# Routing six token tiles of batch 0 to expert slots, and masking six of eight local attention tiles on the vector engine

## Chip, cores and metric

One core of a Trainium2 chip runs the kernel. The metric is the device time of one execution in microseconds (us); lower is better. The engines are PE (matrix products), ACT (scalar functions), DVE (vector operations) and POOL (general operations); SP issues most of the DMAs. Each engine works through its own list of instructions in order and waits on semaphores that others raise.

## The reference, cut to what matters

Input x is 2 batches x 1024 tokens x 128 channels, in fp32. First comes layer norm, an attention of 16 heads of 8 channels and a projection with residual; then layer norm and a gated network of eight experts, of which each token uses two:

```python
# attention: each query sees the 64 keys up to itself, and pooled keys of four levels
As = [S[:, :, qg, kg].reshape(bh, n, m)]          # the local band of 64 keys
...
# gated network
gate_scores = softmax(einsum('btd,ed->bte', x, Wg))
topk_val, topk_idx = top_k(gate_scores, 2)
topk_val = topk_val / (topk_val.sum(axis=-1, keepdims=True) + EPS)
comb = (one_hot(topk_idx, E) * topk_val[..., None]).sum(axis=-2)
for e in range(E):
    a, b = split(einsum('btd,hd->bth', x, W1[e]) + b1[e], 2)
    eo = einsum('bth,dh->btd', a * sigmoid(b), Wo) + bo
    out = out + eo * comb[..., e:e + 1]
```

An expert that a token did not choose has the weight zero in `comb`, so computing all eight for each token and computing only the two chosen give the same output.

## The kernel before

**The order of work** is one list, `schedule()`, written out by hand. Every engine walks the same list (`for step in SCHEDULE`) and does its own part of each step. So a step's place in the list is its place in the order of each engine, and an engine that waits in one step holds up all its later steps.

**Attention** runs in eight units, `u` = 0 to 7: batch `u // 4` and a group of four heads. A unit has ten score steps, `("score", u, i)`. Steps 0 and 1 score all queries against pooled keys (L1289, 8 products each). Steps 2 to 9 score local tile k = i - 2, two windows of 64 queries for four heads: PE first puts the barring values into the bank, a product of 512 columns with the identity (L1303), so that exp gives zero outside the band; then it adds two score products of 256 columns (L1306). ACT takes exp of the bank (L868). Three steps behind, `("out", u, k)` multiplies the probabilities with the values: 16 passes for the local part (L1327) and 4 for the pooled part (L1331). `BARRED_BY_PE` says for which k PE bars; before, it is all eight. For the others DVE has a `mask` step, a minimum of the probabilities with a band that holds the largest number inside and zero outside; before, it never runs. The masks stand in the list one score step behind the score. There are three score banks and a ring of five probability buffers.

Beside these, the list `beside` places other work at a unit and step: projections of q, k, v for later units, the `guard` and `shift` steps of the next unit, and from unit 5 on what ends batch 0: `rden` (DVE's reciprocal of the denominators, L1072), `spread` (DVE multiplies the outputs with reciprocals that went to memory and back, L1078, the DMAs are L576 and L578 in `load_reciprocals`), `proj`, layer norm (`stat2`, `apply2`), `x2T` (transposes), `gatelog` (logits, four steps of six small products) and `gate` in four parts (DVE's top two and weights, L950 to L974). `w1` prepares one expert's weights: POOL subtracts (L724), ACT copies the high part (L841), DVE takes the low part (L1096). `values` lets POOL spread the values of the next half unit (L658, four copies).

**The gated network** follows: 16 tiles of 128 tokens x 8 experts = 128 `hidden` steps. PE makes three products of 512 columns, split in high and low parts (L1140 to L1142), ACT the sigmoid of half of it (L893), DVE the product with the token's weight for this expert (L1123) and POOL adds the experts up (L752). Hidden banks form a ring of five, the temporaries `gtmp` another of five. In the next tile's steps 5 and 7 PE transposes the sum (`hidT`, L1255) and multiplies with the output weights (`y`, L1271). The steps that end batch 1 (`rden`, `spread`, `proj` and so on up to `gate`) are spread over tiles 0 to 7.

**The DMA queue of SP** has its own order, by unit: keys and head queries of the next unit, queries and pooled keys of the one after, weights, and `gather_outputs`, each behind its waits.

## Time and profile before

| | us |
|---|---|
| median of 3 runs | 288.18 (287.26 to 295.06) |
| the profiled execution, time | 288.01 |
| its span, first to last instruction | 286.2 |

Busy in the span: PE 273.4 us (96%), DVE 154.6 (54%), ACT 154.7 (54%), POOL 135.8 (47%). The mean granted clock of PE was 0.964 of full speed. Matrix products overlap their neighbours, so the distance from one start to the next start is what counts for PE, not the printed length of one. PE at 96% busy says that it has few gaps, not that it is at its peak. A length printed for another engine is that of one instruction, or of a run of equal ones with their count behind the x.

### The profile page before, as it was taken

To read this page: it belongs to the slowest core of one execution; us is meant where nothing else is said; L and a number is where in the kernel's file an instruction comes from. 1 tells how busy PE (TensorE), PEld (TensorE's weight loads), DVE (VectorE), ACT (ScalarE), POOL (GpSimd) and SP (SyncE) were. 2 spreads that over 40 slices of the span, in tenths; PEclk is the share of its full clock that TensorE was granted. 3 is DMA by queue.
4 is the path that set the end of the run, shared out by engine and by line. 5 is a ranking of instruction groups with operands and counts; after the bars stand their busy time and mean duration, and the time that the engine had idled before them with its cause. 6 is when DMAs were issued, how large, how long until landed. Compare 5 with 4: busy or idle time off the path is not lost.

```text
span 286.2 us, 7298 instructions
## 1 busy us (share of the span) xinstructions
PE 273.4 (96%) x2705; PEld 226.5 (79%) x2705; DVE 154.6 (54%) x453; ACT 154.7 (54%) x316; POOL 135.8 (47%) x235
## 2 busy tenths in 40 slices
PE   7999999999999999993999999999999999999994
PEld 6868767887788988883888888788888678888883
DVE  7782644633344001322643162789886987777773
ACT  6765745534653432742487456544676555555551
POOL 7753302300041154140171301888885678888881
PEclk9999999989999975998999799999999999999999
DMA  7221176340097687558445011300000000000000
GB/s 212 61 58 60 57 171 192 81 126 2 11 289 277 168 229 170 145 155 165 128 144 154 26 22 21 85 10 10 10 11 9 10 11 10 9 11 18 11 9 19
DMA packets 19683, 24.14 MB, mean 84 GB/s; under 512 B 8312, under 2 KB 14456, under 8 KB 19648
## 3 DMA queue, kind: packets, MB, share of 16 engines
q1 hardware_dynamic: 18528, 22.80, 28.8%
q10 hardware_dynamic: 1120, 0.89, 1.2%
q8 instruction: 21, 0.34, 0.5%
q14 instruction: 14, 0.11, 0.1%
HBM read 11.91 MB, written 5.37 MB: 60 GB/s over the span
## 4 chain that ended last, share of the span: by engine, by line
PE 88%; DVE 3%; issue 3%; DMA 2%; SPq 1%; ACT 1%; POOL 1%; DVEq 0%; ACTq 0%; POOLq 0%
PE bank L1327 13%; PE bank L1140 12%; PE bank L1142 11%; PE bank L1141 11%; PE bank L1303 8%; PE bank L1306 6%; PE bank L1289 5%; PE bank L1221 3%; PE bank L1150 3%; PE bank L1331 2%; PE bank L1271 2%; PE bank L1237 2%; PE bank L1183 1%; DMA qst<-nshiftT 1%; PE bank L1171 1%
## 5 line engine op out<-in xcount | busy, mean ns | idle before, releaser
L752 POOL TENSOR_TENSOR work<-work 128x256 f32<-128x256 f32 x110 | 81.4, 744 | 31.2 <-DVE work L1123 18.3
L1123 DVE SCALAR_TENSOR_TENSOR work<-bank,comb,work 128x256 f32<-128x256 f32 x128 | 58.9, 480 | 24.7 <-ACT work L893 23.4
L893 ACT ACTIVATE work<-bank 128x256 f32<-128x256 f32 x128 | 48.4, 384 | 42.8 <-PE bank L1142 40.3
L868 ACT ACTIVATE work<-bank 128x512 f32<-128x512 f32 x64 | 37.7, 594 | 44.0 <-PE bank L1306 39.8
L1327 PE MATMUL bank<-work,vaug 128*64 128x64 f32 x1024 | 45.7, 235 | 0.0
L1327 PEld LDWEIGHTS bank<-work,vaug 128*64 128x64 f32 x1024 | 37.0, 144 | 9.0 <-issue 1.6
L658 POOL COPY vaug<-vwin 128x64 f32<-128x64 f32 x64 | 13.2, 250 | 51.7 <-PE bank L1331 51.5
L1303 PE MATMUL bank<-bar,ident_r 128*128 128x512 f32 x64 | 34.1, 533 | 0.0
L1306 PEld LDWEIGHTS bank<-qmk,kst 98*128 98x128 f32 x128 | 26.4, 206 | 4.3 <-issue 1.0
L1306 PE MATMUL bank<-qmk,kst 98*128 98x256 f32 x128 | 27.3, 297 | 0.0
L1141 PE MATMUL bank<-arena,xT_hi 128*128 128x512 f32 x64 | 25.1, 392 | 0.0
L1141 PE MATMUL bank<-arena,kst 128*128 128x512 f32 x64 | 25.0, 391 | 0.0
L637 POOL TENSOR_TENSOR rstd<-veps,nhalf 128x4 f32<-128x4 f32 x8 | 8.5, 1064 | 33.3 <-DVE veps L928 33.2
L1048 DVE TENSOR_REDUCE nshift<-bank 128x16 f32<-128x384 f32 x16 | 8.8, 555 | 25.3 <-PE bank L1221 25.3
L1331 PE MATMUL bank<-work,vpool 128*64 128x64 f32 x256 | 18.9, 228 | 0.0
L1289 PE MATMUL bank<-qst,pkm 104*128 104x64 f32 x128 | 17.0, 282 | 0.9 <-DMA qst<-nshiftT 0.9
L1289 PEld LDWEIGHTS bank<-qst,pkm 104*128 104x128 f32 x128 | 15.8, 194 | 1.9 <-ACT work L868 1.0
L863 ACT ACTIVATE work<-bank 128x512 f32<-128x512 f32 x16 | 9.6, 597 | 13.7 <-PE bank L1289 13.7
L1303 PEld LDWEIGHTS bank<-bar,ident_r 128*128 128x128 f32 x64 | 13.1, 204 | 2.8 <-issue 0.5
L724 POOL TENSOR_TENSOR w_stage<-w_stage 128x512 f32<-128x512 f32 x8 | 10.1, 1275 | 7.8 <-DMA w_stage<-w 7.8
L1141 PEld LDWEIGHTS bank<-arena,kst 128*128 128x128 f32 x64 | 12.1, 189 | 2.1
L1331 PEld LDWEIGHTS bank<-work,vpool 128*64 128x64 f32 x256 | 13.5, 144 | 0.0
(217 smaller groups left out, 532.4 us busy)
## 6 DMA issues: line engine op xcount, KB each, us to landing
w_stage<-w SPq DMA_DIRECT2D x8, 512.0 KB, 3.9
qmk<-qst SPq DMA_DIRECT2D x20, 96.0 KB
qst<-arena SPq DMA_DIRECT2D x12, 128.0 KB, 3.8
kst<-arena SPq DMA_DIRECT2D x9, 128.0 KB, 3.2
qst<-q_rows SPq DMA_DIRECT2D x3, 384.0 KB, 4.2
qmk<-q_rows SPq DMA_DIRECT2D x12, 96.0 KB
p_rows<-kpool SPq DMA_DIRECT2D x2, 512.0 KB, 4.5
attT<-denom SPq DMA_DIRECT2D x8, 128.0 KB, 2.8
```

Source lines behind the costliest of these rows:

```text
L752: gp.tensor_tensor(gacc[t % 2][:, :], gacc[t % 2][:, :], gtmp[(adds - 1) % TMP_RING][:, :], ALU.add).then_inc(acc_done, 1)
L868: act.activation(prob[lo % P_RING][:, :, :, :], bank[sc % SCORE_BANKS][:, :].rearrange("p (c j q) -> p c j q", c=2, j=GH), ACT.Exp).then_i ...
L893: act.activation(sig[hn % SIG_RING][:, :], bank[hn % HID_BANKS][:, HID:2 * HID], ACT.Sigmoid).then_inc(sig_done, 1)
L1123: dve.scalar_tensor_tensor(dst[:, :], bank[hn % HID_BANKS][:, 0:HID], comb[:, t, e:e + 1], sig[hn % SIG_RING][:, :], ALU.mult, ALU.mult).t ...
L1140: pe.matmul(out, lhs[0], rhs[0], start=start, stop=False)
L1141: pe.matmul(out, lhs[0], rhs[1], start=False, stop=False)
L1142: return pe.matmul(out, lhs[1], rhs[0], start=False, stop=stop)
L1289: ins = pe.matmul(out[:, k * WIN:(k + 1) * WIN], pkm[s][0:SR + 2 * GH, c, :, :].rearrange("p j k -> p (j k)"), qst[s][0:SR + 2 * GH, c * W ...
L1303: pe.matmul(out[:, :], ident_r[:, :], bar.unsqueeze(1).broadcast_to([P, 2 * GH, WIN]), start=True, stop=False)
L1306: ins = pe.matmul(out[:, k * 256:(k + 1) * 256], kst[s][0:SR + 2, c * WIN:c * WIN + P], qmk[s][0:SR + 2, :, c * WIN:(c + 1) * WIN], start= ...
L1327: pe.matmul(o[e], vaug_flat[hu % 2][:, at:at + VW], prob[lo % P_RING][:, e, j, :], start=(j == 0), stop=False)
L1331: ins = pe.matmul(o[e], vpool_flat[u // NG][:, at:at + VW], probp[u % 2][:, c, :], start=False, stop=True)
```

## The change

**Routing.** `DENSE = 2` tiles of batch 0 and all eight of batch 1 keep the way through all experts. The other six tiles of batch 0 (`ROUTED`) choose two experts per token, 1536 pairs, and each expert's share is padded to whole tiles of 128, at most 19 (`SLOT_TILES`).

- `rank` (unit 7, step 0; PE): 12 small fp32 products that count, for each token and expert, the tokens ahead of it. They wait for the selection that DVE makes in gate part 2.
- `route` (same place; DVE): eleven small operations give each pair its slot (`slot_of`), three more give each slot tile its expert (`expert_of`).
- `scatter` (unit 7, steps 1, 4 and 8; POOL): 3, 3 and 6 indirect DMAs write the normalised rows of 128 tokens to their slots in memory. SP reads the slots back in five DMAs before it broadcasts the reciprocals of batch 1.
- `slotsT` (PE, ACT, DVE): 19 transposes in five groups with high and low parts.
- `slot` (19 of them): PE reads the tile's expert number into a register (`value_load`) and takes the weights at that place; ACT and DVE as in a hidden step, without the token's weight and without POOL. SP stores the result, a ring of four.
- `weigh`, `diag`, `pull` and a new `hidT`: POOL gathers each token's two hidden rows by 12 indirect DMAs (tiles of batch 1, two per routed tile), ACT makes 12 diagonal matrices of the weights, and PE combines and transposes a routed tile by four fp32 products.

**Order.** The steps that end batch 0 move forward, from units 5 to 7 to the end of unit 4 up to unit 6, those that end batch 1 into the last steps of tile 1 and the slots. Expert weights 6 and 7 go from steps 0 and 1 of unit 7 to steps 2 and 4, behind the first and the second scatter. SP copies six experts' high weights beside each other in unit 7. The list's network part is now 16 hidden steps, 19 slots, 64 hidden steps.

**Band.** `BARRED_BY_PE` goes from all eight k to (2, 5); for the other six DVE does the `mask`.

```diff
-BARRED_BY_PE = tuple(range(NB // 2))
+BARRED_BY_PE = (2, 5)
...
-        5: {0: [("rden", 0)], 6: [("spread", 0, 0)], 7: [("spread", 0, 1), ("proj", 0, 0)], 8: [("proj", 0, 1)], 9: [("stat2", 0, 0)]},
-        6: {0: [("stat2", 0, 1)], 1: [("apply2", 0, 0)], 3: [("apply2", 0, 1)], 4: [("x2T", 0, 0)], 8: [("gate weights",), ("x2T", 0, 1)]},
-        7: {0: [("gatelog", 0, 0)], 3: [("gatelog", 0, 1)], 4: [("gatelog", 0, 2)], 5: [("gatelog", 0, 3)],
-            6: [("gate", 0, 0), ("gate", 0, 1)], 8: [("gate", 0, 2)]},
+        4: {9: [("rden", 0)]},
+        5: {3: [("spread", 0, 0), ("spread", 0, 1), ("proj", 0, 0)], 4: [("proj", 0, 1)], 5: [("stat2", 0, 0)], 6: [("stat2", 0, 1)],
+            7: [("apply2", 0, 0)], 9: [("apply2", 0, 1)]},
+        6: {0: [("x2T", 0, 0)], 1: [("gate weights",)], 2: [("x2T", 0, 1)], 4: [("gatelog", 0, 0)], 5: [("gatelog", 0, 1)], 6: [("gatelog", 0, 2)],
+            7: [("gatelog", 0, 3), ("gate", 0, 0)], 8: [("gate", 0, 1)], 9: [("gate", 0, 2)]},
+        7: {0: [("rank",), ("route",)], 1: [("scatter", 0)], 3: [("gate", 0, 3), ("weigh",)], 4: [("scatter", 1)], 8: [("scatter", 2)]},
...
-    for i, (u, at) in enumerate([(4, 6), (4, 8), (5, 6), (5, 8), (6, 5), (6, 7), (7, 0), (7, 1)]):
+    for i, (u, at) in enumerate([(4, 6), (4, 8), (5, 6), (5, 8), (6, 5), (6, 7), (7, 2), (7, 4)]):
...
+        (0, 4): [("rden", 1)], (1, 5): [("hidT", 0)], (1, 6): [("spread", 1, 0), ("spread", 1, 1)], (1, 7): [("y", 0), ("proj", 1, 0)],
+        ("slot", 0): [("proj", 1, 1), ("stat2", 1, 0)], ("slot", 2): [("hidT", 1), ("stat2", 1, 1)], ("slot", 4): [("y", 1), ("apply2", 1, 0)],
+        ("slot", 6): [("apply2", 1, 1)], ("slot", 8): [("x2T", 1, 0)], ("slot", 10): [("x2T", 1, 1)], ("slot", 11): [("gatelog", 1, 0)],
+        ("slot", 12): [("gatelog", 1, 1)], ("slot", 13): [("gatelog", 1, 2)], ("slot", 14): [("gatelog", 1, 3), ("gate", 1, 0)],
+        ("slot", 15): [("gate", 1, 1)], ("slot", 17): [("gate", 1, 2), ("diag",)], ("slot", 18): [("gate", 1, 3)],
...
+            spill_reciprocals(1)
+            sp.wait_ge(slots_sent, 16 * TOPK * ROUTED)
+            sp.wait_ge(vaug_ready, 2 * UNITS)
+            for q in range(SLOT_GROUPS):
+                sp.dma_start(slot_rows[q], slots_dram[4 * q * P:min(4 * q + 4, SLOT_TILES) * P, :].rearrange("(i p) c -> p i c", p=P))\
+                  .then_inc(slots_in[q], 16)
             load_reciprocals(1)
...
+                elif step[0] == "scatter":
+                    if step[1] == 0:
+                        gp.wait_ge(slot_ready, 1)
+                        gp.wait_ge(slots_blank, 16 * SLOT_GROUPS)
+                    for n in range(*SCATTERS[step[1]:step[1] + 2]):
+                        r, k = n // TOPK, n % TOPK
+                        gp.indirect_dma_start(slots_dram, bass.IndirectOffsetOnAxis(ap=slot_of[:, k, r:r + 1], axis=0),
+                                              xnorm[:, DENSE + r, :], None).then_inc(slots_sent, 16)
...
+                elif kind == "rank":
+                    pe.wait_ge(rank_ready, 1)
+                    ones = const[:, C_ONES:C_ONES + P]
+                    for t in range(DENSE, TT):
+                        pe.matmul(bk[:, ROUTED * E:(ROUTED + 1) * E], ones, picked[:, t, :], start=(t == DENSE), stop=(t == TT - 1))
+                    pe.matmul(bk[:, 0:ROUTED * E], const[:, C_EARLIER:C_EARLIER + P], picked[:, DENSE:TT, :].rearrange("p t e -> p (t e)"), start=True, stop=False)
+                    for r in range(ROUTED - 1):
+                        ins = pe.matmul(bk[:, (r + 1) * E:ROUTED * E], ones, picked[:, DENSE + r, :].unsqueeze(1).broadcast_to([P, ROUTED - 1 - r, E]),
+                                        start=False, stop=(r == ROUTED - 2))
...
+                elif kind == "slot":
+                    i = step[1]
+                    if i == 0:
+                        pe.wait_ge(whi_in, 16 * 6)
+                        pe.wait_ge(expert_ready, 1)
+                    pe.wait_ge(hid_done, hn - HID_BANKS + 1)
+                    if i % 4 == 0:
+                        wait_gen_done(pe, ("slotsT", i // 4))
+                    mine = pe.value_load(expert_of[0:1, i:i + 1], min_val=0, max_val=E - 1)
+                    hi, lo = (w[:, bass.ds(mine, 1), :].rearrange("p o n -> p (o n)") for w in (whi, w1T_lo))
+                    ins = split3(bank[hn % HID_BANKS][:, :], tuple(x[i // 4][:, i % 4 * P:(i % 4 + 1) * P] for x in slotsT), (hi, lo))
+                    ins.then_inc(hid_full, 1)
```

## Rows read from the trace of the kernel before

**Rows 1.** Busy time by stretch, with clock and DMA: units 4, 5, 7, the network.

```profile
core 0: us, PE busy (x) PEld busy (x) DVE busy (x) ACT busy (x) POOL busy (x), PEclk, DMA share, GB/s
99.50:118.40 18.90, 18.34 (x212) 15.61 (x211) 3.18 (x8) 8.74 (x15) 8.16 (x17) 0.73 0.68 170
118.40:140.20 21.80, 17.22 (x228) 15.04 (x226) 6.39 (x13) 8.26 (x14) 3.25 (x6) 0.92 0.63 164
...
154.90:173.80 18.90, 18.90 (x289) 16.61 (x285) 7.33 (x46) 8.79 (x16) 4.01 (x10) 0.91 0.16 45
173.80:286.20 112.40, 107.94 (x540) 88.08 (x538) 83.87 (x227) 62.10 (x160) 84.19 (x116) 1.00 0.06 17
```

**Rows 2.** Timeline of PE in attention: start, length, engine, line, operation, count.

```profile
116.98 0.50 PE L1303 MATMUL bank<-bar,ident_r 128*128 128x512 f32 x1
117.31 0.40 PE L1306 MATMUL bank<-qmk,kst 98*128 98x256 f32 x2
117.64 0.69 PE L1327 MATMUL bank<-work,vaug 128*64 128x64 f32 x16
118.16 0.29 PE L1331 MATMUL bank<-work,vpool 128*64 128x64 f32 x4
118.37 1.97 PE L1289 MATMUL bank<-qst,pkm 104*128 104x64 f32 x16
120.18 0.48 PE L1303 MATMUL bank<-bar,ident_r 128*128 128x512 f32 x1
```

**Rows 3.** Timeline of all engines in the network, rows of PE.

```profile
240.59 0.38 PE L1255 MATMUL bank<-const,work 128*128 128x128 f32 x2
...
240.72 0.47 PE L1140 MATMUL bank<-qmk,kst 128*128 128x512 f32 x1
...
242.19 0.61 PE L1271 MATMUL bank<-woT,work 128*128 128x128 f32 x4
...
242.55 0.48 PE L1140 MATMUL bank<-kpool,kst 128*128 128x512 f32 x1
...
246.80 0.38 PE L1255 MATMUL bank<-const,work 128*128 128x128 f32 x2
```

**Rows 4.** The costliest groups of the page: busy us, mean ns, idle before them.

```profile
L752 POOL TENSOR_TENSOR work<-work 128x256 f32<-128x256 f32 x110 | 81.4, 744 | 31.2 <-DVE work L1123 18.3
L1123 DVE SCALAR_TENSOR_TENSOR work<-bank,comb,work 128x256 f32<-128x256 f32 x128 | 58.9, 480 | 24.7 <-ACT work L893 23.4
L893 ACT ACTIVATE work<-bank 128x256 f32<-128x256 f32 x128 | 48.4, 384 | 42.8 <-PE bank L1142 40.3
L868 ACT ACTIVATE work<-bank 128x512 f32<-128x512 f32 x64 | 37.7, 594 | 44.0 <-PE bank L1306 39.8
```

**Rows 5.** The chain that ended last: start, us, what.

```profile
39.30 3.67 DMA qst<-nshiftT
...
100.53 2.65 DMA pkm<-p_rows
...
129.57 4.58 issue
```

**Rows 6.** One line's instructions (L1078, then L724): shortest, median, longest in ns.

```profile
L1078 DVE TENSOR_TENSOR attT<-attT,vpool x4: 681/688/1228, 133.4 to 191.2; 128x512 f32<-128x512 f32 x4
...
L724 POOL TENSOR_TENSOR w_stage<-w_stage x8: 1267/1276/1282, 110.7 to 158.3; 128x512 f32<-128x512 f32 x8
```

**Rows 7.** DMA issues: SP's timeline, line L526, then KB and us to landing.

```profile
116.11 0.59 SPq L568 DMA_DIRECT2D attT<-denom  x1
...
179.83 0.33 SPq L576 DMA_DIRECT2D r_rows<-dcomp  x1
181.40 0.59 SPq L578 DMA_DIRECT2D vpool<-r_rows  x1
...
L526 SPq DMA_DIRECT2D pkm<-p_rows x16: 759/776/1547, 50.7 to 132.2; - x16
...
attT<-denom SPq DMA_DIRECT2D x8, 128.0 KB, 2.8
...
vpool<-r_rows SPq DMA_DIRECT2D x2, 512.0 KB, 4.7
```

**Rows 8.** Timeline of DVE: the gate of batch 0.

```profile
166.62 0.17 DVE L1108 COPY glog<-bank 128x16 f32<-128x16 f32 x1 [1.90 <-PE bank L1142]
...
169.47 0.22 DVE L964 TENSOR_REDUCE gsum<-gexp 128x8 f32<-128x64 f32 x1
...
170.35 0.22 DVE L968 TENSOR_TENSOR gexp<-gexp,gsel 128x64 f32<-128x64 f32 x1
...
171.57 0.22 DVE L974 TENSOR_REDUCE csum<-comb 128x8 f32<-128x64 f32 x1
```

**Rows 9.** Timeline of PE in the prologue: small fp32 products.

```profile
11.72 0.97 PE L1171 MATMUL bank<-const,xnorm 128*128 128x30 f32 x8
12.53 0.64 PE L1163 MATMUL bank<-const,xnorm 128*128 128x128 f32 x4
```

More of the change, by code:

```diff
@@ L60 @@
 TOPK = 2
+DENSE = 2
+ROUTED = T // P - DENSE
+SLOT_TILES = (ROUTED * P * TOPK + E * (P - 1)) // P
+SLOT_GROUPS = (SLOT_TILES + 3) // 4
 LN_EPS, GATE_EPS = 1e-5, 1e-9
```

240 lines of the change are left out of this document (193 added, 47 removed).

## The prediction

> **What bounds the kernel now.** I read the page first, then busy time by stretch, then the chain that ended last, then the timelines of PE, DVE, POOL and SP. The first stretches are the eight attention units; the last unit ends at 173.8, and everything after is the gated network, 112.4 us long [rows 1]. PE is busy in nearly all of it. So time is PE's time plus the few places where PE waits, and the question for each edit is whether it shortens PE's list or makes PE wait.
>
> In attention a step of PE is 1.39 us: the barring product takes 0.33 from its start to the next start, the two local score products 0.33, the sixteen passes of the value product 0.52 and the pooled ones 0.21 [rows 2]. In the network a tile of eight experts is 6.21 us from one transpose to the next; two transposes make 0.21 of it (0.13 and 0.08 more until the next product is at pace), the four output passes 0.45 (0.36 and 0.09), and what is left is 5.55, or 0.69 a step [rows 3]. ACT needs 0.384 for its part of a step, DVE 0.480 and POOL 0.744 for seven of eight [rows 4], so all fit under a tile.
>
> The chain shows three waits of PE outside this: DMA for the shift rows at the start of unit 1, DMA of the pooled keys at 100.5, and 4.58 us at 129.6 before the projection, which waits for the broadcast of the reciprocals [rows 5].
>
> **What is removed.** Hidden steps go from 128 to 80 dense and 19 slots: 29 fewer, 29 x 0.69 = 20.0 us of PE. Barring products go from 64 to 16: 48 fewer. One takes 0.33, but it hides the weight load of the product behind it; if that comes bare about 0.05 to 0.1 returns, so the bounds are 0.23 (a 512-column product at pace in the network) and 0.33. I take 0.28: 13.4 us, and about five of them ran at half clock (unit 4 was granted 0.73 of full speed, so it spent 10 us of 18.9 at the lower level, some four steps, and unit 7 one), 1.4 more. Together 14.8.
>
> **What is not kept of the 14.8.** The pooled keys of unit 5 arrive by a chain of spills and loads that starts late in unit 2 and does not get shorter; about eight removed products lie beside it, so 2.2 us become waiting there. The shift rows at unit 1 likewise: 1.0. Masks are now on DVE: 48 of 128x512 with both inputs in SBUF, 0.688 by the median of such a product [rows 6], 33 us in all where DVE is at 40% or less. Between a score and its use lie three steps, some 3.3 us, and exp 0.594 and mask 0.688 need 1.5 with semaphores. So a mask is late only behind other DVE work above 1.5 us. I take 1.0 for it (bounds 0 and 6: one mask late by about 1 us in each of units 1 to 6).
>
> The Trainium skill (SBUF — State Buffer, section Who interferes with whom) says that a two-input DVE product from SBUF and a POOL operation that reads SBUF lock each other out. The longest of the four such products, 1.228 against a median of 0.688, ran beside POOL's additions, which agrees [rows 6]. By that rule a mask could wait for the whole of a 1.276 weight subtraction, still inside the slack; it adds nothing to the sum.
>
> **Moved: projection of batch 0.** The reciprocal goes to the end of unit 4 and the multiply to step 3 of unit 5. Denominators are issued at 116.11 and land 2.8 later, about when unit 5 starts (118.37); the reciprocal itself, the spill, 1.6 us until the broadcast may be issued, and 4.7 to its landing follow [rows 7]: with the multiply, about 9 us after the unit's start. PE wants it after two first scores of 0.9 [rows 2], two steps of 1.1 and 0.6 of guard products, 4.6. So PE waits some 4.5 us, as it does now (4.58). Zero, bounds -2 and +2. SP stands in this wait ahead of unit 6's keys and queries, which have over 8 us to spare.
>
> **Added in units 6 and 7.** Ranking needs the gate of batch 0 at the start of unit 7. From the last logit copy (166.62) to the selected gates (end 170.57) DVE takes 3.95 [rows 8]; one mask and one weight subtraction of 0.69 now lie between: 5.4. PE has two steps of 1.1 and the first score of 0.9 there, 3.1, so it waits 2.3. The rank products are 12 in fp32, 24 passes of 0.10 (8 passes in 0.81) [rows 9]: 2.4.
>
> After them DVE's route: 11 small operations at 0.23 (nine gaps from 169.47 to 171.57 make 2.1) [rows 8], slots known after 2.7. POOL stands in this wait; behind it three scatters, the values of unit 7 (0.9) and the subtraction of expert 6's weights (1.28). ACT stands in order at its copy of these weights, and the exps behind it; DVE at its own part, and the masks behind it. No row shows an indirect DMA. The bounds are 0.33, the shortest DMA issue seen, and 1.547, the longest; the nearest kind, a scattered load of many short rows, has a median of 0.776 [rows 7]. I take 0.8. Then: 2.7 + 2.4 + 0.9 + 1.28 + ACT 0.6 + DVE 0.69 + mask 0.69 = 9.3 for the first value product, which PE reaches after 4.9 (a first score of 0.9, three steps of 1.1, one barring product and a score). The second three scatters and expert 7: POOL free at 7.3 + 2.4 + 1.28 = 11.0, exp and mask after it 13.0, for the value product of step 8 that PE reaches after 8.5 (3.6 later). So unit 7 waits 4.5 in all, of which the six scatters are 4.8: at 0.33 a scatter it would be 1.7, at 1.547 9.0. The six scatters of step 8 are off the path.
>
> **Added in the network.** Nineteen transposes of slots at 0.10: 1.9. Combining a routed tile takes eight fp32 passes of 0.09 in place of two transposes of 0.21: 0.5 x 6 = 3.1. The diagonals, twelve small ACT passes in a row at slot 17, delay the sigmoids by some 3 us against a ring of five banks: 1.0.
>
> The second projection moves from step 20 to step 15. The spill of the reciprocals is issued at 179.83, which is 6.0 after the network's start; five slot loads of 1.2 MB are now issued (0.6 each) before the broadcast, which took 4.7 alone [rows 7]. It lands at about 6.0 + 3.6 + 4.7 + 1.1 (behind the slot loads) = 15.4, the multiply takes 0.7, and PE is there at 16 x 0.69 + 0.66 = 11.7: a wait of 4.4. After the wait of 4.58 in unit 5 the granted clock averaged 0.92 over 21.8 us, so 3.5 us were at the lower level (1.2 instead of 2.4 GHz) and cost 1.7 [rows 1]; the same again here. Together 6.1, bounds 0 and 9.
>
> Each slot loads its expert number into a register of PE's queue before its products. No row shows this. Nothing is the lower bound: five banks are 3.45 us of products, sigmoid and product take 0.86 of that [rows 4], so there is time for a lookup under products already issued, if PE's queue does that. The upper is 1.57, a small DMA's way out and back (179.83 to 181.40) [rows 7], of which 1.2 might stay bare: 23 us. I take 0.2 a slot, 4.0, nearer to the lower one, because PE is busy in 107.94 of 112.40 us of the network, so its queue issues without gaps [rows 1].
>
> The Trainium skill (DMA: Bandwidth & Descriptors, section Latency and other measured facts) gives a floor of about 600 ns for a tensor load. If none of it were hidden, the term would be 11.4 in place of 4.0 and the time 291, an estimate from that page; no row here shows it.
>
> POOL's pulls: per tile 7 x 0.744 + 2 x 0.8 = 6.8 against PE's 7.2: it fits, and only the first pull, behind the last slot's store, costs 0.5.
>
> **The sum.** Attention: -14.8 + 2.2 + 1.0 + 1.0 + 2.3 + 2.4 + 4.5 = -1.4. Network: -20.0 + 1.9 + 3.1 + 1.0 + 6.1 + 4.0 + 0.5 = -3.4. The profiled execution took 288.0 (span 286.2 and 1.8 around it); less 4.8 is 283.2, say 283. Its own time is the median of the runs (288.18) within 0.2, so nothing is shifted.
>
> **Rivals.**
> - *Cheap issue (0.26).* Scatters cost 0.35 and the register load is hidden. For it: PE's queue issues without gaps in the network, and 0.33 was seen for a DMA issue. Against it: short rows cost more in every issue seen. 6 x 0.45 + 4.0 = 6.7 less: 277.
> - *The waits are not there (0.07).* The second projection finds its broadcast in time, or unit 7 its slots; another 5 less: 272.
> - *The register paces the slots (0.13).* Slower than before. At 0.8 unhidden a slot (half the upper bound) 15.2 us in place of 4.0: 294. It decides from 0.7 a slot on. Against it: the ring's slack.
> - *Descriptor work binds POOL (0.13).* At 1.55 a DMA unit 7 waits 4.5 more, and a tile needs 5.2 + 3.1 = 8.3 against 7.2, six times: 6.6. 294. It decides from about 1.5; against it stands only the median of 0.776.
> - *DVE masks late (0.07).* The barring gain goes into waits for masks, 5 more than taken: 288.
> - *My forecast (0.34).* 279 to 288, the terms near the values taken.
>
> **Chances.** About 2% is what a measurement here can tell from no change: from the median below 282.4 is faster, above 293.9 slower. Faster: 0.08 of the forecast, 0.24 and 0.07 of the first two, 0.39. Slower: 0.26. Within: 0.35. The range reaches from between the first two rivals to beyond the slower ones: 271 to 299.
>
> **What would show it.** Right: hidden steps of 0.69 still; PE waiting 2 to 3 us before the rank products and about 5 in unit 7 with ACT on POOL's weight subtraction; a wait of 4 us before the first projection of batch 1; unit 7 ending near 172.4. Wrong: slots more than 1 us apart (register), scatters below 0.5 or above 1.3, value products waiting for DVE's masks in units 1 to 5, or the lower clock for more than 25 us in all.

## The result and the profile after

The kernel became slower, far beyond the range of the forecast.

| | before | after |
|---|---|---|
| median of 4 runs each, us | 291.0 (287.26 to 295.06) | 334.42 (329.52 to 341.14) |
| ratio, 95% interval | | 1.1532 (1.1342 to 1.1723) |
| profiled execution: span, us | 286.2 | 339.3 |
| its mean granted clock of PE | 0.964 | 0.787 |

The ratio and its interval, here and below, go by the fast runs alone, those within 1.5% of the fastest of the same kernel; medians go by all runs.

Section 1 of the page of the kernel after (busy time, share, instructions) and the row of the granted clock in 40 slices of the span:

```profile
PE 302.3 (89%) x2649; PEld 252.0 (74%) x2649; DVE 177.9 (52%) x493; ACT 150.7 (44%) x304; POOL 134.7 (40%) x217
...
PEclk9999965859969595585555555797696799999999
```

The same row of the kernel before:

```profile
PEclk9999999989999975998999799999999999999999
```

Of the two levels, 2.4 and 1.2 GHz, the engine spent 2 x (1 - 0.787) x 339.3 = 144.5 us at the lower one; before it was 2 x 0.036 x 286.2 = 20.6 us. PE has fewer instructions than before (2649 against 2705) and is busy 29 us longer, because each takes longer at the lower level. And it is idle for 37.0 us (339.3 less 302.3) where it was for 12.8: 24 us more. The loss of 53 us in span is the sum of the two. The profiled execution has the lowest clock of this kernel's runs; the others had 0.809 to 0.843.

Busy time by stretch of the kernel after: units 4, 5, 6 and 7, then the network (columns as in [rows 1]):

```profile
107.90:125.10 17.20, 16.95 (x206) 14.55 (x205) 6.02 (x11) 8.64 (x15) 9.25 (x17) 0.70 0.67 172
125.10:155.00 29.90, 20.54 (x221) 18.09 (x219) 12.74 (x36) 9.00 (x17) 8.34 (x17) 0.64 0.43 109
155.00:183.70 28.70, 28.70 (x238) 25.75 (x236) 11.79 (x49) 11.53 (x23) 3.37 (x6) 0.50 0.30 87
183.70:216.60 32.90, 28.60 (x282) 25.43 (x281) 14.11 (x39) 8.18 (x15) 18.01 (x22) 0.52 0.29 96
...
216.60:339.30 122.70, 104.81 (x506) 84.11 (x504) 70.66 (x203) 57.91 (x148) 64.64 (x86) 0.91 0.20 59
```

Unit 5 was 21.8 us long and unit 7 18.9 [rows 1]; they are 29.9 and 32.9. Unit 6 has no wait of PE at all, and is 28.7 long at a clock of 0.50, half speed from end to end. The network, with 29 hidden steps fewer, is 122.7 against 112.4. So attention lost 42.8 us (216.6 against 173.8) and the network 10.3. In the network PE is idle for 17.9 us where it was for 4.5, and the clock was 0.91 in place of 1.00.

What PE waited for in the kernel after, the three longest sums (sum, times, longest):

```profile
PE bank L1403 <- issue: 9.6, 2, 5.1
PE bank L1528 <- DVE work L1223: 8.9, 4, 4.9
PE bank L1424 <- DMA vaug<-hidden_rows,slot_of: 4.1, 6, 1.6
```

They stand at the two projections (L1403), value products whose masks come late (L1528) and the products that take the hidden rows pulled for routed tiles (L1424). "issue" before L1403 is a wait for something that the profile does not name; the broadcast of the reciprocals lies there.

### The profile page after: what moved, and what is told of

Read it like the earlier page. It is cut to its first block, busy times and chain, and to the rows that moved or that the text cites. A ratio compares the mean times of both kernels' runs of the same rounds, so it can differ in the third digit from the quotient of the medians.

```text
span 339.3 us, 7238 instructions
## 1 busy us (share of the span) xinstructions
PE 302.3 (89%) x2649; PEld 252.0 (74%) x2649; DVE 177.9 (52%) x493; ACT 150.7 (44%) x304; POOL 134.7 (40%) x217
## 4 chain that ended last, share of the span: by engine, by line
PE 62%; POOL 12%; DVE 9%; issue 8%; ACT 5%; DMA 3%; POOLq 0%; ACTq 0%; DVEq 0%
PE bank L1528 12%; PE bank L1306 7%; POOL work L860 6%; PE bank L1308 6%; PE bank L1307 6%; PE bank L1507 5%; PE bank L1490 4%; PE bank L1387 4%; POOL vaug L852 3%; PE bank L1316 3%; PE bank L1403 2%; PE bank L1532 2%; DVE work L1223 2%; PE bank L1504 2%; DMA vaug<-hidden_rows,slot_of 2%
## 5 line engine op out<-in xcount | busy, mean ns | idle before, releaser
L1528 PE MATMUL bank<-work,vaug 128*64 128x64 f32 x1024 | 59.3, 279 | 8.9 <-DVE work L1223 8.9
L1528 PEld LDWEIGHTS bank<-work,vaug 128*64 128x64 f32 x1024 | 49.0, 185 | 20.5 <-DVE work L1223 9.9
L860 POOL TENSOR_TENSOR work<-work 128x256 f32<-128x256 f32 x68 | 50.1, 738 | 17.1 <-DVE work L1279 8.9
L1011 ACT ACTIVATE work<-bank 128x256 f32<-128x256 f32 x99 | 37.4, 384 | 41.7 <-PE bank L1308 36.7
L1279 DVE SCALAR_TENSOR_TENSOR work<-bank,comb,work 128x256 f32<-128x256 f32 x80 | 36.6, 479 | 29.7 <-POOL work L860 16.0
L1223 DVE TENSOR_TENSOR work<-work,const 128x512 f32<-128x512 f32 x48 | 35.9, 756 | 9.8 <-ACT work L976 9.7
L1507 PE MATMUL bank<-qmk,kst 98*128 98x256 f32 x128 | 40.3, 407 | 0.0
L842 POOL DMA_INDIRECT slot_rows<-xnorm,slot_of x12 | 12.6, 1050 | 27.0 <-DVE slot_of L1114 23.9
L852 POOL DMA_INDIRECT vaug<-hidden_rows,slot_of x12 | 11.6, 969 | 27.0 <-DMA hidden_rows<-vaug 24.5
L1203 DVE TENSOR_REDUCE nshift<-bank 128x16 f32<-128x384 f32 x16 | 8.8, 555 | 18.0 <-PE bank L1387 17.9
L1403 PE MATMUL bank<-wproj,attT 128*128 128x128 f32 x32 | 8.1, 434 | 9.6 <-issue 9.6
L1387 PE MATMUL bank<-pkm,qst 96*128 96x96 f32 x64 | 14.5, 368 | 2.3 <-issue 1.7
```

Of the source, the lines that this page charges most:

```text
L860: gp.tensor_tensor(gacc[DENSE_AT[t] % 2][:, :], gacc[DENSE_AT[t] % 2][:, :], gtmp[(adds - 1) % TMP_RING][:, :], ALU.add).then_inc(acc_done, 1)
L1011: act.activation(sig[hn % SIG_RING][:, :], bank[hn % HID_BANKS][:, HID:2 * HID], ACT.Sigmoid).then_inc(sig_done, 1)
L1223: dve.tensor_tensor(tile, tile, band.unsqueeze(1).broadcast_to([P, 2 * GH, WIN]), ALU.min).then_inc(mask_done, 1)
L1279: dve.scalar_tensor_tensor(dst[:, :], bank[hn % HID_BANKS][:, 0:HID], comb[:, t, e:e + 1], sig[hn % SIG_RING][:, :], ALU.mult, ALU.mult).t ...
L1387: ins = pe.matmul(bk[:, i * GK:(i + 1) * GK], qst[u % 2][0:SR, t * P:(t + 1) * P], pkm[u % 2][0:SR, 2 * t, :, POOLED:LK], start=True, stop ...
L1507: ins = pe.matmul(out[:, k * 256:(k + 1) * 256], kst[s][0:SR + 2, c * WIN:c * WIN + P], qmk[s][0:SR + 2, :, c * WIN:(c + 1) * WIN], start= ...
```

## The experiments

**How runs are compared.** The clock differs from run to run of one kernel: 39 runs of the kernel before, beside the experiments, lay between 0.903 and 0.988, and their times between 281.87 and 305.16. The product of span and clock is steadier. The last column gives its median, "full-clock us": a microsecond at the lower level counts a half. For these 39 runs it was 272.7 to 277.2. It is no measure of time, and it counts a wait at the lower level half as well, though a wait would not get shorter at the higher one. But it separates how much there is to do from how fast it was done.

| kernel | time, us | before beside it, us | clock, range of its runs | full-clock us, median |
|---|---|---|---|---|
| before, 18 runs | 291.99 | | 0.925 to 0.988 | 275.7 |
| after | 334.42 | 291.0 | 0.787 to 0.843 | 273.6 |
| band only | 301.2 | 292.89 | 0.865 to 0.930 | 265.8 |
| band, barring products kept | 292.99 | 292.89 | 0.932 to 0.982 | 278.4 |
| routing only | 329.75 | 292.89 | 0.845 to 0.905 | 281.8 |
| batch 0's end moved only | 298.61 | 293.96 | 0.930 to 0.954 | 279.2 |
| before with fillers | 292.12 | 293.96 | 0.948 to 0.982 | 279.2 |
| routing with fillers | 326.85 | 293.96 | 0.922 to 0.934 | 301.7 |
| routing, weights first (three runs) | 323.37 | 293.96 | 0.856 to 0.899 | 285.7 |
| routing, plain scatters | 316.82 | 297.21 | 0.887 to 0.928 | 282.7 |
| routing, plain pulls | 323.17 | 291.99 | 0.858 to 0.897 | 281.2 |
| routing, broadcast first | 324.11 | 291.99 | 0.868 to 0.933 | 286.0 |
| reciprocals first | 284.08 | 291.99 | 0.932 to 1.000 | 273.4 |
| reciprocals first, with fillers | 284.45 | 291.99 | 0.935 to 0.994 | 273.7 |

The profiled executions tell more exactly where time went, since a trace has the stretches of the lower level and PE's busy time in them:

| profiled execution | span, us | PE idle | PE busy | of it at the lower level |
|---|---|---|---|---|
| before | 286.2 | 12.8 | 273.4 | 20.1 |
| band only | 301.5 | 15.2 | 286.3 | 75.1 |
| band, barring products kept | 289.9 | 15.6 | 274.3 | 23.7 |
| batch 0's end moved only | 293.4 | 18.0 | 275.4 | 25.8 |
| routing only | 330.1 | 33.3 | 296.8 | 90.6 |
| routing with fillers | 327.1 | 29.7 | 297.4 | 48.9 |
| after | 339.3 | 37.0 | 302.3 | 128.7 |

### Each half of the change alone

`band_only` is the kernel before with one line changed, `route_only` the kernel after with that line changed back:

```diff
# band_only, from the kernel before
-BARRED_BY_PE = tuple(range(NB // 2))
+BARRED_BY_PE = (2, 5)
# route_only, from the kernel after
-BARRED_BY_PE = (2, 5)
+BARRED_BY_PE = tuple(range(NB // 2))
```

> The kernel before with BARRED_BY_PE = (2, 5) and nothing else changed: no routing, 48 barring products fewer, 48 masks on DVE. Theory A (the lost products cost the clock): the sum of products alone would give 13 us less, but PE is granted the lower clock in most of units 1 to 7; mean clock below 0.87, 305 to 320 us. Rival B (masks come late on DVE): slower too, 290 to 305, with the clock at 0.95 or more and PE waiting for DVE's masks for over 10 us. Rival C (the band is what I forecast, all the loss is in routing): 273 to 282.

> The changed kernel with all eight local tiles barred by PE, as before: routing and the moved steps alone. Theory A: the clock stays high in units 0 to 5 (first five units as long as before within 3 us); the rest of the loss is in unit 7 and the network: 300 to 312 us, mean clock over 0.92. Rival B: the same numbers, so this run does not tell A from B. Rival C: as slow as the changed kernel, 325 or more.

Measured beside a median of 292.89 for the kernel before (281.87 to 300.78, 7 runs): band only 301.2 (292.65 to 306.83), routing only 329.75 (314.8 to 333.62). Each is slower, by 8.3 and by 36.9, and the two add up to 45.2 where both together cost 43.4 (334.42 against 291.0). So routing has four fifths of the loss.

`band_only` took the time of rival B but not its mechanism: PE waits 0.3 us in all for masks, and the clock is 0.875 in the profiled execution, near what theory A said. `route_only` took the time of rival C: 325 or more, with the clock at 0.855 where theory A wanted 0.92. So the lost barring products are no explanation of the greater part.

### The band with its products kept

`band_filler` keeps the six masks of DVE, and PE still makes all eight barring products, which the first score product now overwrites. So DVE does what it does in `band_only`, and PE what it does before:

```diff
-                        if barred:
-                            if u == 0:
-                                pe.wait_ge(bar_ready, 1)
-                            pe.matmul(out[:, :], ident_r[:, :], bar..., start=True, stop=False)
+                        if u == 0:
+                            pe.wait_ge(bar_ready, 1)
+                        pe.matmul(out[:, :], ident_r[:, :], bar..., start=True, stop=not barred)
```

> As band_only, but PE still makes the 48 barring products into the score bank, where the first score product overwrites them (start), so they compute nothing that is used: PE's columns as before, masks on DVE. Theory A: the clock comes back (0.95 or more) and the time is that of the kernel before, 286 to 294. Rival B: PE still waits for masks and the time is that of band_only or longer, 300 or more.

Measured: 292.99 (286.02 to 301.04), against 292.89 of before and 301.2 of `band_only`. Units 2 and 3 of `band_only`, by stretch:

```profile
64.30:86.40 22.10, 22.10 (x226) 17.76 (x225) 10.53 (x23) 10.97 (x20) 3.00 (x9) 0.77 0.14 34
86.40:107.90 21.50, 19.86 (x357) 17.40 (x356) 11.18 (x18) 8.56 (x15) 4.63 (x7) 0.84 0.76 241
```

The same units of `band_filler`:

```profile
63.70:84.10 20.40, 20.40 (x231) 16.09 (x230) 10.69 (x24) 11.69 (x21) 3.19 (x9) 0.92 0.19 52
84.10:104.30 20.20, 18.81 (x366) 16.41 (x362) 11.04 (x18) 7.98 (x14) 4.44 (x7) 1.00 0.74 243
```

DVE's load is the same in both (10.5 against 10.7, 11.2 against 11.0). With the products kept, units 2 and 3 are shorter although PE makes at least five more in each, because the clock is 0.92 and 1.00 in place of 0.77 and 0.84. In unit 2 of `band_only` PE has no gap (22.10 of 22.10), and yet the clock is low: what had changed in PE's list is that 512-column products were gone. The timeline of PE in unit 3 of `band_only`, at one of the two k that PE still bars, shows what a step costs at the lower level:

```profile
95.72 0.76 PE L1303 MATMUL bank<-bar,ident_r 128*128 128x512 f32 x1
96.28 0.63 PE L1306 MATMUL bank<-qmk,kst 98*128 98x256 f32 x2
96.84 1.12 PE L1327 MATMUL bank<-work,vaug 128*64 128x64 f32 x16
97.75 0.43 PE L1331 MATMUL bank<-work,vpool 128*64 128x64 f32 x4
98.11 0.42 PE L1230 MATMUL bank<-const,nshift_parts 128*64 128x128 f32 x1
```

From the start of L1303 to that of the product behind L1331 it takes 2.39 us (95.72 to 98.11), against 1.39 [rows 2]. Without its product such a step is 1.83 (2.39 less 0.56, an estimate), 0.44 longer at 1.2 GHz than one with the product at 2.4.

So the masks are not what costs, and the barring products paid for themselves (clocks of 0.932 to 0.982 with them and 0.865 to 0.930 without, four runs each): the work saved is there (265.8 full-clock us against 276.2 for the runs of before beside it, 10.4 less) and is spent on the clock. That leaving the products out lowers the clock is shown by these two kernels; the inner reason, how the chip decides, is not.

### The steps of batch 0 moved forward, alone

`moved_only` is the kernel before with batch 0's end at the places of the change (projection in unit 5, step 3, gates at the end of unit 6), SP's broadcast issued at the end of unit 4's block as there, without routing:

```diff
-        5: {0: [("rden", 0)], 6: [("spread", 0, 0)], 7: [("spread", 0, 1), ("proj", 0, 0)], ...
+        4: {9: [("rden", 0)]},
+        5: {3: [("spread", 0, 0), ("spread", 0, 1), ("proj", 0, 0)], 4: [("proj", 0, 1)], ...
```

> The kernel before (no routing, all eight tiles barred by PE) with only the steps that end batch 0 moved forward as in the change, expert weights 6 and 7 left at steps 0 and 1 of unit 7. Theory A: the moved steps themselves cost: a wait of 5 to 8 us before the projection in unit 5, a second one of about 5 us while POOL makes rstd and then a weight subtraction that ACT waits for, and then the lower clock through unit 6 and part of 7; 12 to 22 us more than before, 304 to 314. Rival D: the loss in units 5 to 7 is the ranking, the scatters and their DMAs: this kernel is within 4 us of before.

Measured: 298.61 (295.18 to 300.77), before 293.96 beside it, ratio 1.0351 (1.0179 to 1.0524). So the moved steps alone cost 4.7 us by the medians and 5 to 15 by the ratio, where the forecast had the move of the projection at nothing. By the medians that is less than the 12 to 22 of theory A and just above the 4 that rival D allowed; the interval reaches into theory A's range. Unit 5 is 27.6 long (117.6 to 145.2) with a clock of 0.75 and a wait of 6.6 for the projection; PE is idle for 18.0 us in place of 12.8.

### More products to hold the clock

`before_fill` and `route_fill` add products of 512 columns (the barring product again) whose results are overwritten, where PE waits or makes small ones:

```diff
+FILL = {('pl', 1): 2, ('xT', 1, 1): 3, ('v', 1, 1): 3, ('guard', 5, 0): 2, ('proj', 0, 0): 18, ('gatelog', 0, 0): 3}
...
+                for _ in range(FILL.get(step, 0)):
+                    pe.matmul(bk[:, :], ident_r[:, :], bar..., start=True, stop=True)
```

> The kernel before with 31 more products of 512 columns, overwritten by the step's own: 18 in the wait before the projection of unit 5, the rest in stretches of short products ahead of the four places where the clock fell (start of unit 2, end of unit 3 and start of 4, start of unit 7). Theory A: the work costs 13 x 0.23 = 3 us and the clock no longer falls, which is worth up to 9.5 us: mean clock 0.98 or more and 282 to 288 by time. Rival E (the clock falls for another reason than few columns): clock as before, 3 us more.

> route_only with products of 512 columns that are overwritten: 20 in the wait before the projection of unit 5, 16 in the wait before x2T, 3 before each logit step of unit 6, a few before the guards of unit 7, 8 before the ranking. Theory A: units 6 and 7 run at the high clock for most of their length and take 12 to 20 us less, less about 5 us for the work: 315 to 322. Rival D (waits for DVE, POOL and DMAs set units 6 and 7): the clock comes back and the time stays within 4 us of route_only, 329.75.

`before_fill`: 292.12 against 293.96, ratio 1.0102 (0.9832 to 1.0372), no difference that can be told, with the clock at 0.948 to 0.982 against 0.925 to 0.964 beside it; neither theory A's 282 to 288 nor rival E's 3 us more can be read from it. `route_fill`, with fillers at fifteen places of routing only (twenty at the projection, sixteen at the transposes): 326.85 (321.11 to 328.99), with the clock at 0.922 to 0.934. Against 329.75 of routing only that is 3 us, though the clock is back to near that of before. The fillers themselves lengthened PE's list (301.7 full-clock us against 281.8). So fillers cost here about what they bring: the time stayed within 4 us of routing only, as rival D said. It is still 33 us slower than the kernel before, with a clock near that one's. The 74 fillers are at most 17 of these (an estimate, at 0.23 each, the pace of a product in the network), so some 16 us are neither fillers nor, with the clocks so near, the clock; PE is idle for 29.7 us, 16.9 more than before.

### The two weight subtractions ahead of the scatters

```diff
-    for i, (u, at) in enumerate([(4, 6), (4, 8), (5, 6), (5, 8), (6, 5), (6, 7), (7, 2), (7, 4)]):
+    for i, (u, at) in enumerate([(4, 6), (4, 8), (5, 6), (5, 8), (6, 5), (6, 7), (7, 0), (7, 0)]):
```

> route_only with expert weights 6 and 7 prepared at step 0 of unit 7, ahead of the first scatter, so that ACT and DVE wait for no scatter. My reckoning of unit 7: 5 to 9 us less than route_only (twice three scatters at 1.27), that is 320 to 325 against 329.75, with unit 7 waiting on the values behind a scatter at most. Rival A': unit 7 is set by the lower clock and PE's own work, not by these waits: less than 3 us gained.

Measured: 328.46 (one of its four runs took 818 us and is left out of what follows; the other three 320.85 to 333.56). Units 5 to 7 took 80.3 us in its profile against 87.7 in routing only. But unit 7, where the edit lies, did not get shorter: it took 32.4 us (166.9 to 199.3) at a clock of 0.74, against 29.5. What got shorter is unit 6, 21.2 at 0.84 against 29.7 at 0.56, in which the code is the same. So the 5 to 9 us that were expected of unit 7 are not there. Rival A' had the gain right but not all of the reason: in this unit 7 PE now waits 2.2 us for the gate, and POOL 4.4 us for the weights' DMA.

### Scatters and pulls by plain DMAs

`scatter_plain` (from routing only) takes the 12 indirect DMAs off POOL; SP writes the same rows to fixed slots, behind the same wait:

```diff
+                    sp.wait_ge(slot_ready, 1)
+                    sp.wait_ge(slots_blank, 16 * SLOT_GROUPS)
+                    for n in range(TOPK * ROUTED):
+                        sp.dma_start(slots_dram[n * P:(n + 1) * P, :], xnorm[:, DENSE + n // TOPK, :]).then_inc(slots_sent, 16)
...
-                elif step[0] == "scatter":
...
```

> Routing alone (all tiles barred by PE), with POOL's 12 scatters replaced by 12 plain DMAs of SP that write the same rows to fixed slots, behind the same wait for the slots. The combined rows of six tiles of batch 0 are therefore not those of the tokens' own experts; the size and number of the transfers stay. POOL no longer stands in unit 7 for the slot numbers nor for 1.27 us a scatter. Theory S (the scatters hold back the weight subtractions and through ACT and DVE the value products of unit 7): unit 7, 29.5 us long in routing alone, gets shorter by about 6 (six scatters of 1.27 of the path, less what the exps leave), ACT's waits of 5.59 and 3.80 for POOL's subtraction go, and unit 7 is some 23 long. Theory H (PE at its half clock needs the time anyhow: unit 7 before took 18.9 at 0.91 of full speed and would take about 31 at 0.55): unit 7 stays within 2 us of 29.5 while the granted clock stays near 0.55. The network's length stays at 120.5 by both, and the time near 323 by S and 329 by H.

Measured: 316.82 (309.34 to 321.59), the clock 0.887 to 0.928; before beside it 297.21 (282.21 to 305.16). The time is below both theories. Its units 6 and 7 by stretch:

```profile
149.40:170.60 21.20, 20.64 (x241) 18.36 (x241) 7.41 (x28) 13.19 (x28) 5.61 (x15) 0.84 0.42 123
170.60:195.00 24.40, 22.43 (x290) 19.83 (x287) 8.45 (x48) 8.72 (x16) 3.69 (x6) 0.79 0.42 132
```

The same units of routing only:

```profile
150.40:180.10 29.70, 29.16 (x242) 25.58 (x242) 9.29 (x48) 13.43 (x28) 4.29 (x10) 0.56 0.33 94
180.10:209.60 29.50, 27.36 (x288) 24.34 (x287) 6.48 (x27) 8.09 (x15) 16.28 (x22) 0.64 0.29 100
```

Unit 7 went from 29.5 to 24.4, near the 23 of theory S, and ACT's wait for POOL's subtraction (8.6 us in routing only) is no longer among its waits. But the clock rose too, which it should not have done by theory H. A third run settles how much is whose: `pull_plain` (below) has the same unit 7 as routing only, with its scatters, and had there the clock of `scatter_plain`:

```profile
178.60:208.10 29.50, 24.46 (x288) 20.98 (x287) 6.47 (x27) 8.26 (x15) 16.29 (x22) 0.79 0.30 103
```

It is 29.5 long at 0.79 as at 0.64: with the scatters the length of unit 7 did not follow the clock, because the chain over POOL set it. At equal clock the scatters and what waits for them cost 5.1 us there.

Unit 6 went from 29.7 to 21.2, all of it by a clock of 0.84 for 0.56, and nothing was changed in it. Its code is the same in five profiles: it took 29.7, 30.1 and 30.1 us in `route_only`, `pull_plain` and `rden_before_slots`, at a clock of 0.55 to 0.56, and 21.2 in `scatter_plain` and in `w1_first`, at 0.84. `w1_first` keeps all scatters, so they are not what lowers the clock there; what does is open.

`pull_plain` (from routing only) replaces the 12 gathers of POOL by plain DMAs of SP:

```diff
-                        gp.indirect_dma_start(pulled[r % 2][k], None, hidden_dram,
-                                              bass.IndirectOffsetOnAxis(ap=slot_of[:, k, r:r + 1], axis=0)).then_inc(pulled_in[r % 2], 16)
+                        sp.dma_start(pulled[r % 2][k], hidden_dram[(2 * r + k) * P:(2 * r + k + 1) * P, :]).then_inc(pulled_in[r % 2], 16)
```

> route_only with the 12 gathers of POOL replaced by 12 plain DMAs of SP that read fixed rows of the slots' results, so the combined rows of six tiles are not the tokens' own; everything else is computed. It takes 2 x 1.27 us a tile off POOL. Theory F (POOL sets the last 64 hidden steps: 7 additions and 2 gathers, 8.4 us a tile, where PE needs about 7): the part from the first hidden step of batch 1 to the end falls from 72 to 60 to 63 us, 318 to 321 by time. Rival G (PE's eight fp32 passes a tile and the clock set it): it stays above 69.

Measured: 323.17 (317.16 to 327.09). The part of the network that belongs to batch 1 went from 72.4 us to 67.2, by 5.2, between the 60 to 63 of theory F and the 69 of rival G. In the kernel after, POOL's timeline of one such tile:

```profile
290.73 0.97 POOL L852 DMA_INDIRECT vaug<-hidden_rows,slot_of  x1
292.00 0.95 POOL L852 DMA_INDIRECT vaug<-hidden_rows,slot_of  x1 [0.30 <-issue]
292.95 6.04 POOL L860 TENSOR_TENSOR work<-work 128x256 f32<-128x256 f32 x7
299.14 0.97 POOL L852 DMA_INDIRECT vaug<-hidden_rows,slot_of  x1
```

A tile takes 8.41 us (290.73 to 299.14), and POOL is idle in it for less than 0.5: 1.27 from the first gather to the second, 0.95 for that, 6.04 for seven additions (0.86 each) and 0.15 to the next gather. PE's timeline in `pull_plain`:

```profile
291.43 1.05 PE L1423 MATMUL bank<-vpool,vaug 128*128 128x128 f32 x8
...
293.70 0.60 PE L1471 MATMUL bank<-woT,work 128*128 128x128 f32 x4
...
298.97 1.05 PE L1423 MATMUL bank<-vpool,vaug 128*128 128x128 f32 x8
```

Without the gathers a tile takes 7.54 (291.43 to 298.97), and PE sets it: 6.21 [rows 3], the eight passes of the routed tile's product (0.80 and 0.09) and its four output passes (0.45) make 7.55. So POOL bound the last part, at 0.87 us a tile; six such tiles are the 5.2. Theory F had PE at about 7 and so expected twice that.

### The broadcast ahead of the slot loads

```diff
+            load_reciprocals(1)
             for q in range(SLOT_GROUPS):
                 sp.dma_start(slot_rows[q], ...
-            load_reciprocals(1)
```

> route_only with SP issuing the broadcast of batch 1's reciprocals ahead of the five slot loads instead of behind them. If the slot loads ahead of it cause PE's wait before the second projection (3.5 us in route_only), that wait falls below 1 us and the time by 2 to 4; but the slots then come later, and if slotsT is what is late next, the gain turns into a wait before slot 0 and the time stays.

Measured: 324.11 (311.16 to 328.57), its clocks reaching from 0.868 to 0.933 where those of routing only were 0.845 to 0.905. PE's timeline in the kernel after shows the wait and what follows it:

```profile
228.08 0.61 PE L1472 MATMUL bank<-woT,work 128*128 128x128 f32 x4
233.81 2.05 PE L1403 MATMUL bank<-wproj,attT 128*128 128x128 f32 x8 [5.13 <-issue]
235.66 1.91 PE L1452 MATMUL bank<-const,vwin 128*128 128x128 f32 x8
239.18 0.79 PE L1306 MATMUL bank<-qmk,pkm 128*128 x1 [1.61 <-DVE pkm L1291]
```

5.13 is the wait for the broadcast (forecast: 4.4), and behind the transposes of the slots the first slot waits 1.61 more for their copies on ACT and DVE. In routing only the two are 3.54 and 1.61. With the broadcast first they are 1.24 (expected: below 1) and 1.63, another of 0.58 for DVE comes between, and the slots start 7.0 us after the last dense step of batch 0 instead of 10.0. That is 3.0 us, within the 2 to 4 expected; the medians lie 5.6 apart, of which the clock has a part that these runs do not separate (full-clock us rose, from 281.8 to 286.0).

### Reciprocals first, in the kernel before

The same idea in the kernel before, at its one long wait (4.58 before the projection [rows 5]): SP issues the broadcast of batch 0's reciprocals at the start of unit 5's block, ahead of the keys and queries of unit 6.

```diff
             for u in range(1, UNITS):
+                if u == NG + 1:
+                    load_reciprocals(0)
                 if u + 1 < UNITS:
                     load_keys(u + 1)
...
-                if u == NG + 1:
-                    load_reciprocals(0)
```

> The kernel before with one edit: at the start of unit 5 SP spills and broadcasts the reciprocals of batch 0 ahead of unit 6's keys and head queries. The 4.58 us in which PE waits before the projection go, and the fall of the clock behind it (1.7 us): 4 to 6 us less than before. If the other loads become late instead, unit 6 starts with a wait and the time stays within 1 us.

Measured: 284.08 (276.57 to 294.43, 8 runs) against 291.99 (18 runs), ratio 0.9704 (0.9509 to 0.9899). PE's timeline at the projection:

```profile
128.03 0.29 PE L1331 MATMUL bank<-work,vpool 128*64 128x64 f32 x4
129.87 0.95 PE L1237 MATMUL bank<-wproj,attT 128*128 128x128 f32 x3 [1.56 <-issue]
```

The wait is 1.56 in place of 4.58. In full-clock us the kernel has 273.4 against 275.7, near the 3 us of the wait; a run at 276.57 had a clock of 1.00 throughout. By the medians it is 7.9 us faster than before, where 4 to 6 were expected; the interval leaves 1 to 5%.

`rden_fill` adds three fillers at a projection of v and two at unit 5's guard:

```diff
+FILL = {('v', 1, 1): 3, ('guard', 5, 0): 2}
```

> rden_first with five more products of 512 columns that are overwritten: three ahead of the last value projection at the end of unit 3, two before the first guard product of unit 5. Theory A: the fall of the clock over 10 us in unit 4 goes (worth up to 5 us for 1.2 us of work): 2 to 4 us less than rden_first, clock 0.98. Rival E: 1 us more than rden_first.

Measured: 284.45 (279.98 to 291.85, 12 runs), ratio 0.9894 (0.9811 to 0.9977). Against 284.08 without them the gain of 2 to 4 that theory A promised is not there, and the clocks are alike (0.935 to 0.994 against 0.932 to 1.000). The fillers add nothing that can be told; the version without them is the one to keep.

## Why the prediction was wrong

**The step that failed is the clock.** The prediction had two terms for the lower level, 1.7 more and 1.4 less, and took every other step of PE at the pace it had before. It named the sign itself: the lower clock for more than 25 us in all. It was 144.5 us, and PE was busy for 128.7 of these, against 20.1 before. A busy microsecond there would take a half at the higher level at best (two rows read at both levels: 2.39 us became 1.39, a slot's product 0.43 became 0.23). That makes the lower level 46 to 54 us dearer than before (0.42 to 0.50 of 108.6, an estimate), where the forecast had 0.3.

**The waits were too small by less.** PE's waits were forecast 16.9 us longer (2.2 + 1.0 + 1.0 + 2.3 + 4.5 in attention, 1.0 + 4.4 + 0.5 in the network); its idle time is 24.2 longer.

**The sum of the work was close.** The products that go and come, with the register's 4.0, were forecast at -22.0 (-13.4 - 20.0 + 2.4 + 1.9 + 3.1 + 4.0); with the clock's share taken off, PE's busy time changed by -17 to -25 (28.9 more in all, less those 46 to 54). The full-clock us agree too (273.6 against 275.7, where -4.8 was forecast; band -10.4 for -10.6, routing +5.6 for +5.8), but that is partly luck, since waits at the lower level count half in it and the idle time was larger than forecast.

What is shown of the cause, and what not: that the clock falls when the barring products go is shown by `band_only` and `band_filler`, for some 8 of the 43 us. That routing made PE wait 20 us more, and run at the lower level for 70 busy us more, stands in its profile. Why the clock falls there, by its waits, its small products or something else, was not isolated and stays open.

**Barring products.** 0.28 us each was right at 2.4 GHz. That nothing else would change when 48 of them go was not written down as a step, and it was wrong (`band_only`, `band_filler`). A rival on the clock was missing; the largest rival price was +11.

**Masks.** 0.684 in the median, as forecast (0.688), but four came late, 8.9 us in all, where 1.0 was taken. By the timeline three are long: 4.89 in unit 5, 1.82 and 1.94 in unit 7; units 1 to 4 have one of 0.25. (In unit 3 two masks in a row push a DVE product of the pooled values back, for which PE waits 1.68.) The longest, in unit 5, hangs on the moved layer norm. DVE, POOL and ACT of the kernel after in order of time:

```profile
145.74 1.39 POOL L727 TENSOR_TENSOR rstd<-veps,nhalf 128x4 f32<-128x4 f32 x1 [20.38 <-DVE veps L1047]
...
150.03 2.48 POOL L814 TENSOR_TENSOR w_stage<-w_stage 128x512 f32<-128x512 f32 x2
151.32 0.63 ACT L949 ACTIVATE wqkv_parts<-w_stage 128x512 fp32r<-128x512 f32 x1 [3.87 <-POOL w_stage L814]
151.99 1.07 DVE L1251 TENSOR_TENSOR arena<-w_stage,wqkv_parts 128x512 fp32r<-128x512 f32 x1 [4.34 <-ACT wqkv_parts L949]
152.98 0.72 DVE L1223 TENSOR_TENSOR work<-work,const 128x512 f32<-128x512 f32 x1
153.75 0.48 PE L1528 MATMUL bank<-work,vaug 128*64 128x64 f32 x4 [4.89 <-DVE work L1223]
```

POOL stands 20.38 us waiting for the layer norm of batch 0, whose place is now ahead of the weight subtraction; the subtraction comes late, ACT and DVE wait for it in order, and the mask and PE's value product are last. DVE had less room than the prediction took, too: it read 40% or less, but in units 1 and 6 of the kernel before it was busy for 8.55 of 17.30 and 7.29 of 14.70 us. The prediction followed this very chain in unit 7 and not in unit 5, where it put the moved steps at zero. The first wait itself was right in size: 4.47 before the projection, against a forecast of 4.5; but in routing only it was 7.4 and in `moved_only` 6.6. `moved_only` shows that the moved steps cost something without any routing, though it kept the weight subtractions of unit 7 in their places.

**Unit 7.** The chain was the one forecast, and PE waits there for 4.3 us in all (0.54 before the rank products, where 2.3 was forecast, and 1.82 and 1.94 for masks behind the scatters, where 4.5 was); the rest of its 32.9 is PE at a clock of 0.52. POOL and ACT of the kernel after:

```profile
194.13 1.22 POOL L842 DMA_INDIRECT slot_rows<-xnorm,slot_of  x1 [23.93 <-DVE slot_of L1114]
195.66 0.96 POOL L842 DMA_INDIRECT slot_rows<-xnorm,slot_of  x1 [0.30 <-issue]
196.93 0.96 POOL L842 DMA_INDIRECT slot_rows<-xnorm,slot_of  x1 [0.30 <-issue]
...
198.62 1.26 POOL L814 TENSOR_TENSOR w_stage<-w_stage 128x512 f32<-128x512 f32 x1
199.92 0.63 ACT L949 ACTIVATE qmk<-w_stage 128x512 fp32r<-128x512 f32 x1 [5.59 <-POOL w_stage L814]
```

A scatter was 1.27 us from start to start (1.050 long by the mean of 12) where 0.8 was taken; six of them on the path are 2.8 more. The slots were known 2.4 us after the products (forecast 2.7). The rank products took 5.3 us (186.10 to 191.40) for 2.4, at half clock. The unit ended at 216.6, not near 172.4.

**Slots.** The register term of 4.0 was wrong by all of it: no cost of it can be seen. In the kernel after, two slots at full clock:

```profile
244.54 0.48 PE L1306 MATMUL bank<-qmk,pkm 128*128 x1
244.85 0.40 PE L1307 MATMUL bank<-arena,pkm 128*128 x1
245.09 0.40 PE L1308 MATMUL bank<-qmk,pkm 128*128 x1
245.32 0.40 PE L1306 MATMUL bank<-qmk,pkm 128*128 x1
```

The second slot starts 0.78 after the first, of which 0.31 is the first product behind a transpose, as in a dense tile [rows 3]; the other products are 0.23 apart, the pace of a dense step. The Trainium skill (DMA: Bandwidth & Descriptors, section Latency and other measured facts) gives about 600 ns for a tensor load; by these rows nothing of it lies bare, so the estimate of 291, which took all of it as bare, does not hold here.

**Pulls.** "It fits" was wrong: POOL takes 8.41 us a tile and PE 7.55, not 6.8 and 7.2. The rival on descriptor work had the right engine, place and size of a tile (8.3), and set its point of decision too high, at 1.5 us a DMA: with additions at 0.86 instead of 0.744 it was 0.75 a gather (7.55 less 7 x 0.863, over two). 0.744 is the length of one instruction [rows 4]; from start to start it is more, and the trace of the kernel before has that too. Its timeline of POOL, 18 additions in a row, 0.85 each:

```profile
239.31 15.28 POOL L752 TENSOR_TENSOR work<-work 128x256 f32<-128x256 f32 x18
```

**Second projection.** 5.13 for a forecast 4.4. Unforecast was the way from the transposes over ACT and DVE to the first slot, 3.5 us from 235.66 to 239.18, of which PE is idle for 1.61.

## What to carry to other kernels

A sum over PE's instructions holds only at the clock of the profile it was read from. When a change takes wide products away, or puts waits and small products in their place, price the stretch at both levels as a rival of its own: here some 20 us less work came with 43 us more time. The clock of a stretch can differ between two profiles of the same code, so an edit's effect on a stretch is read between runs with the same clock there. And when a step moves forward in a list that all engines walk in order, write out for each engine what now stands behind its wait, in every unit that it passes; the cheapest gain is often a transfer issued one place earlier on its queue.

## What the runs showed of the hardware

- The granted clock fell without any gap of PE, and for longer when 512-column products were left out: unit 2 0.92 before and 0.77 in `band_only`, busy without a gap in both. With the products made again, and overwritten, it was 0.92.
- The same code ran at 0.55 of full clock in three profiles and at 0.84 in two (unit 6 of the routing kernels, 30 us or 21).
- One kernel's time varied with its clock and little else: 276.57 us at 1.00 and 294.43 at 0.932 for `rden_first`.
- An indirect DMA of 128 rows held POOL for 0.95 to 1.36 us (medians 0.972 and 0.958), and the next mostly began 1.27 after its start, for scattered rows of 512 bytes and gathered ones of 1024 alike. Weights taken by an index in a register of PE came at the pace of fixed ones, 0.23 us a product.
- A mask that ran beside POOL's scatter and subtraction took 2.37 us, against a median of 0.684, and the four copies of POOL behind it 2.21 against 0.76. DVE and POOL of the kernel after:

```profile
203.02 0.97 POOL L842 DMA_INDIRECT slot_rows<-xnorm,slot_of  x1 [0.30 <-issue]
...
203.51 2.37 DVE L1223 TENSOR_TENSOR work<-work,const 128x512 f32<-128x512 f32 x1
204.02 1.27 POOL L814 TENSOR_TENSOR w_stage<-w_stage 128x512 f32<-128x512 f32 x1
205.22 2.21 POOL L748 COPY vaug<-vwin 128x64 f32<-128x64 f32 x4
```

The Trainium skill (SBUF — State Buffer, section Who interferes with whom) says that a DVE product with two inputs in SBUF and a POOL operation that reads SBUF contend for the read interface that they share; by that rule, the trace agrees.
